# Merged expert and scan block of layer 2: key and decay rows spread to 128 partitions by transfers, value and query spreads of two steps in one round

## What is computed

```
x = x + L2_attn(xn) + L2_ffn(xn)
# L2_attn, per head and for every pair (i, j) of the 8 x 8 state, over the sequence:
state[t] = keep[t] * state[t-1] + (gate[t] * k[t])_i * v[t]_j
y[t]_j  = sum_i q[t]_i * state[t]_ij
# L2_ffn, per expert:
out = square(relu(x @ c_fc[e])) @ c_proj[e]
```

## Time and profile before

| | |
|---|---|
| median of the runs (lowest, highest) | 2280.9 us (2278.33, 2287.1) |
| profiled execution, its own time | 2283.21 us |
| its span | 2281.3 us |
| mean granted TensorE clock | 0.91 |
| busy share of the span: PE, DVE, ACT, POOL | 84%, 73%, 54%, 23% |
| merged block, first matmul to the next block's first | 1295.6 to 1518.7 us |

### The profile page before, as it was taken

How to read it: one execution, slowest core, us unless ns; L and a number is a source line. 1 busy time by engine, 2 the same in 40 slices (tenths; PEclk the granted TensorE clock), 3 DMA queues, 4 the chain that set the end, 5 groups by cost and what they waited for, 6 DMA issues and landing times. The chain is left out here.

```text
span 2281.3 us, 45278 instructions
## 1 busy us (share of the span) xinstructions
PE 1918.8 (84%) x17589; PEld 991.8 (43%) x17589; DVE 1669.8 (73%) x2861; ACT 1221.0 (54%) x2473; POOL 517.9 (23%) x602
## 2 busy tenths in 40 slices
PE   2888877866647999999978899999897988697899
PEld 1222221443211337943342377766443455565554
DVE  5999999685779996579854755537675887685665
ACT  3999999332324884368854255555342031184433
POOL 1112110012674551134425533320100000001100
PEclk7898999987776999999988899999998999987999
DMA  8423420100642524624211122220124242000000
GB/s 276 84 56 84 84 56 1 74 18 6 152 165 39 126 44 120 189 56 78 31 22 56 58 66 65 63 97 1 62 91 128 82 118 73 8 1 27 1 19 19
DMA packets 150333, 159.39 MB, mean 70 GB/s; under 512 B 53580, under 2 KB 123030, under 8 KB 150114
## 3 DMA queue, kind: packets, MB, share of 16 engines
q1 hardware_dynamic: 139880, 140.43, 22.7%
q0 software_dynamic: 10240, 16.06, 3.2%
HBM read 87.53 MB, written 72.82 MB: 70 GB/s over the span
## 5 line engine op out<-in xcount | busy, mean ns | idle before, releaser
L435 ACT ACTIVATE a_E<-a_scores,a_nmax 128x512 f32<-128x512 f32 x512 | 343.2, 814 | 14.6 <-DVE a_nmax L368 13.7
L1014 ACT ACTIVATE a_E<-a_scores 128x512 f32<-128x512 f32 x512 | 273.5, 601 | 96.4 <-PE a_scores L1049 91.3
L368 DVE TENSOR_REDUCE a_nmax<-a_scores 128x2 f32<-128x1024 f32 x256 | 302.6, 1217 | 21.8 <-PE a_scores L450 18.1
L918 DVE TENSOR_REDUCE a_nmax<-a_first 128x2 f32<-128x1024 f32 x256 | 295.5, 1217 | 15.2 <-PE a_first L1039 14.1
L450 PE MATMUL a_scores<-a_Vh,a_Kh 48*128 48x512 bf16 x512 | 108.2, 421 | 96.5 <-ACT a_E L435 71.9
L1039 PE MATMUL a_first<-a_Kh,a_Qh 48*128 48x512 bf16 x512 | 148.1, 416 | 36.9 <-PEq L51 20.1
L463 PE MATMUL a_turn<-a_E,a_QS 128*32 128x256 f32 x2048 | 174.1, 416 | 2.3 <-DVE a_QS L378 1.8
L435 ACT ACTIVATION_READ_ACCUMULATOR a_E<-a_scores,a_nmax 128x1 f32 x512 | 167.1, 335 | 0.0
L1049 PE MATMUL a_scores<-a_Qh,a_Kh 51*128 51x512 bf16 x512 | 160.7, 394 | 5.1 <-PEq L51 1.9
L1071 PE MATMUL a_out<-a_E,a_V 128*32 128x256 f32 x2048 | 161.7, 396 | 0.0
L450 PEld LDWEIGHTS a_scores<-a_Vh,a_Kh 48*128 48x128 bf16 x512 | 24.9, 94 | 216.5 <-ACT a_E L435 179.1
(11 more groups left out here) (546 smaller groups left out, 4409.4 us busy)
## 6 DMA issues: line engine op xcount, KB each, us to landing
f_up<-in_L_up SPq DMA_DIRECT2D x32, 256.0 KB, 3.3
a_Kh<-a_rows_k SPq DMA_DIRECT2D x16, 384.0 KB, 6.3
a_Vh<-a_rows_v SPq DMA_DIRECT2D x16, 384.0 KB, 9.8
a_Qh<-a_rows_q SPq DMA_DIRECT2D x32, 192.0 KB, 5.1
a_Kh<-a_rows_k SPq DMA_DIRECT2D x32, 192.0 KB, 6.1
slots<-empty SPq DMA_DIRECT2D x8, 645.0 KB, 6.4
f_xe<-slots SPq DMA_DIRECT2D x40, 129.0 KB, 2.0
outs<-zeros SPq DMA_DIRECT2D x8, 512.0 KB, 5.8
```

The costliest lines, as they stand in the source:

```text
L368: v.tensor_reduce(nmax[:, rd % 2, r1, :, q], bank(b, u)[:], AX.X, ALU.max, negate=True).then_inc(S["max_ready"], 1)
L435: m = a.activation(E[:, u % NE, x], bank(b, u)[:, x], ACT.Exp, bias=nmax[:, rd % 2, r1, x, q:q + 1], accum_out=Z[:, rd % 2, r1, x, q:q + 1])
L918: v.tensor_reduce(out, slot_bank(n)[:], AX.X, ALU.max, negate=True).then_inc(S["slot_read"], 1)
L1014: a.activation(E[:, u % NE, x], ps_s[n % 3][:], ACT.Exp, scale=SCALE).then_inc(S["exp_ready"], 1)
```

## The change

- The spreads of key and decay by TensorE go, with ScalarE's copy of the key and its three buffers, and the PSUM tiles ps_k and ps_d.
- SyncE issues a transfer for each in their place, `expand(i)`. It reads 16 rows of gk (or keep) in SBUF, each eight times, and writes 128 partitions of 512 float32. The destination is the array g.XT, which has no other use at this time: columns 0 to 3 of NB for keys, 4 to 7 for decays, so there are NX = 4 buffers of each. `at` is the first of the 16 rows: 96, 0, 32, 64, 112, 16, 48, 80 over the eight steps of a batch.
- The first four steps' transfers, eight in all, stand ahead of the wait for `put` and of the loads of tiles 0 and 1. After that, one pair (for step t+4) stands ahead of the load of tile t+3. The key's waits for product t (its buffer), the decay's for scan t.
- ps_v and ps_q have two buffers. On even s, TensorE spreads q(s), v(s+1), q(s+1), v(s+2) in one round; on odd s it spreads nothing.
- VectorE's product and scan take key and decay from SBUF, in place of a2m_gk_e and PSUM.

```diff
+                def expand(i):
+                    if i < ALL:
+                        b, t = first + i // NT, ORDER[i % NT]
+                        at = 32 * ((t // 2 + 3) % 4) + 16 * (t % 2)
+                        if i % NT == 0 and b >= GATED_EARLY:
+                            sp.wait_ge(S["gated"], b - GATED_EARLY + 1)
+                        if i >= NX:
+                            sp.wait_ge(S["kv_done"], i - NX + 1)
+                        sp.dma_start(key_rows[:, i % NX], mix["gk"][at:at + 16, b].unsqueeze(1).broadcast_to([16, 8, T])
+                                     ).then_inc(key_at[i % NX], 16)
+                        if i >= NX:
+                            sp.wait_ge(S["scanned"], i - NX + 1)
+                        sp.dma_start(decay_rows[:, i % NX], mix["keep"][at:at + 16, b].unsqueeze(1).broadcast_to([16, 8, T])
+                                     ).then_inc(decay_at[i % NX], 16)
+
+                for i in range(NX):
+                    expand(i)
                 sp.wait_ge(put, 16 * 2 * NB * R)
                 load(0)
                 load(1)
                 ahead(sp)
                 load(2)
                 for t in range(TILES):
+                    expand(t + NX)
                     load(t + 3)
...
                 for s in range(TILES):
-                    if s < ALL:
-                        spread_dq(s)
+                    if s % 2 == 0:
+                        spread_q(s)
                         spread_v(s + 1)
-                        spread_k(s + 2)
+                        spread_q(s + 1)
+                        spread_v(s + 2)
...
-                        v.tensor_tensor(kv[:, i % 2], gk_e[:, i % 3], ps_v[:], ALU.mult).then_inc(S["kv_done"], 1)
+                        v.tensor_tensor(kv[:, i % 2], key_rows[:, i % NX], ps_v[i % 2][:], ALU.mult).then_inc(S["kv_done"], 1)
...
-                    v.tensor_tensor_scan(state[:, i % NS], ps_d[:], kv[:, i % 2], 0.0, ALU.mult, ALU.add
+                    v.tensor_tensor_scan(state[:, i % NS], decay_rows[:, i % NX], kv[:, i % 2], 0.0, ALU.mult, ALU.add
                                          ).then_inc(S["scanned"], 1)
```

More of the change, by code:

```diff
@@ L2105, in experts_and_scan2 @@
         hr = k.sb("f2_hr", [128, 2, NF, TS])
-        gk_e, kv = k.sb("a2m_gk_e", [128, 3, T]), k.sb("a2m_kv", [128, 2, T])
+        kv = k.sb("a2m_kv", [128, 2, T])
+        NX = NB // 2
+        key_rows, decay_rows = g.XT[:, 0:NX], g.XT[:, NX:2 * NX]
+        key_at, decay_at = ([g.sem(f"f2m_{n}_at{i}") for i in range(NX)] for n in ("key", "decay"))
         NS = NT + 1
         state = k.sb("a2m_state", [128, NS, T])
-        ps_k, ps_v, ps_d, ps_q = (k.ps(f"a2m_ps_{n}", [128, T]) for n in "kvdq")
+        ps_v, ps_q = ([k.ps(f"a2m_ps_{n}{i}", [128, T]) for i in range(2)] for n in "vq")
         ps_x, ps_y = k.ps("f2_ps_x", [128, T]), k.ps("f2_ps_y", [128, T])
@@ L2112, in experts_and_scan2 @@
         S = {n: g.sem(f"f2m_{n}") for n in ("x_turned", "xT_ready", "h_done", "r_ready", "h_ready", "y_done", "y_ready",
-                                            "gated", "k_spread", "v_spread", "expanded", "k_read", "kv_done", "scanned",
+                                            "gated", "v_spread", "kv_done", "scanned",
                                             "state_ready", "picked", "sum_read", "q_spread", "row_ready")}
@@ L2160, in spread, with spread_q @@
                     return pe.matmul(ps[:], sel[rows, t % 2], mix[name][rows, b], start=True, stop=True)
[L2162 to L2169, removed]
                 def spread_v(i):
                     if i < ALL:
[L2173 to L2181, removed]
+                        if i >= 2:
+                            pe.wait_ge(S["kv_done"], i - 1)
+                        spread(ps_v[i % 2], "v", selJ, i, 1).then_inc(S["v_spread"], 1)
+                def spread_q(i):
+                    if i < ALL:
+                        if i >= 2:
+                            pe.wait_ge(S["state_ready"], i - 1)
+                        spread(ps_q[i % 2], "q", selI, i, 0).then_inc(S["q_spread"], 1)
                 def add_up(b):
@@ L2245, in _ @@
             def _(a):
[L2246 to L2249, removed]
-                            a.wait_ge(S["kv_done"], i - 2)
-                        a.copy(gk_e[:, i % 3], ps_k[:]).then_inc(S["k_read"], 1)
                 def sum_out(b):
@@ L2271, in out @@
                     a.copy(ye[:, t % 2].rearrange("p h c -> p (h c)"), ps_y[:, 0:2 * C]).then_inc(S["y_ready"], 1)
-                copy(0)
-                copy(1)
                 for s in range(TILES):
-                    copy(s + 2)
                     if s % NT == 0 and 0 < s <= ALL:
@@ L2292, in product @@
                     if i < ALL:
-                        v.wait_ge(S["k_read"], i + 1)
+                        v.wait_ge(key_at[i % NX], (i // NX + 1) * 16)
                         v.wait_ge(S["v_spread"], i + 1)
@@ L2296, in product @@
                             v.wait_ge(S["scanned"], i - 1)
-                        v.tensor_tensor(kv[:, i % 2], gk_e[:, i % 3], ps_v[:], ALU.mult).then_inc(S["kv_done"], 1)
+                        v.tensor_tensor(kv[:, i % 2], key_rows[:, i % NX], ps_v[i % 2][:], ALU.mult).then_inc(S["kv_done"], 1)
                 def scan(i):
-                    v.wait_ge(S["expanded"], i + 1)
+                    v.wait_ge(decay_at[i % NX], (i // NX + 1) * 16)
                     v.wait_ge(S["kv_done"], i + 1)
@@ L2309, in weigh @@
                     v.wait_ge(S["q_spread"], i + 1)
-                    v.tensor_tensor(state[:, i % NS], state[:, i % NS], ps_q[:], ALU.mult).then_inc(S["state_ready"], 1)
+                    v.tensor_tensor(state[:, i % NS], state[:, i % NS], ps_q[i % 2][:], ALU.mult).then_inc(S["state_ready"], 1)
                 def take(t):
```

2 lines of the change are left out of this document (removed).

## The result

The changed kernel takes 2325.6 us (median of 4 runs, 2316.8 to 2329.4), the kernel before 2284.0 us beside it: a ratio of 1.0177, 95% interval 1.0150 to 1.0203, so 41.6 us slower. The profiled execution took 2327.34 us, with a span of 2325.5.

The account below looks back on a forecast made before the run. TensorE's work was taken to bound the merged block. Rounds -21.4, start +13.0 and shortage +9.0 summed to +0.6 us on 2283.2, giving 2283.8; the median, 2.3 us lower, was forecast at 2281.5 us, range 2258 to 2311.

Parts of the forecast that it names:

- Rounds: TensorE's spread rounds in the merged block: 20 instead of 40, each 1.07 us, saving 21.4 us; mean step 4.66 us.
- Transfer: One key or decay transfer reading 16 SBUF rows: 2.28 us at 115 GB/s, between bounds of 0.72 and 4.7 us.
- Start: At the merged block's start, eight transfers stand before tile 0's load, so its turn comes 13.0 us late.
- The shortage in steady steps: Transfers plus other traffic exceed a step by 1.00 us; a quarter, 0.25 us, is lost over 36 steps: 9.0 us.
- SyncE's queue: Two more issues of 0.49 us each step before the load of tile t+3; the queue is not held longer.
- The bound rival: Transfers of 2.28 us bound the merged block without overlap: steps of 5.66 us, 36.0 us lost, 2308.5 us; chance 0.32.
- (1): Sign in the merged block: 20 rounds of 1.07 us and odd steps of 3.93 us where nothing waits.
- (2): Sign at the block's start: first turn some 13 us after 1303, with TensorE waiting for the load of xe.
- (3): Sign on the pairs: issue to landing over 4 us, growing where the queue backs up; under 3 us if hidden.
- (4): Sign in the merged block: a DMA share near 1, from 0.24.
- (5): Sign in the merged block: TensorE's waits for xe or the scan's for its decay sum to about 9 us.
- the remote 4.7 us: Remote case: a transfer takes 4.7 us by rate per source partition, a step 10.5 us, some 200 us slower; chance 0.03.

Follow-up runs that it names:

- The HBM version: The change with gk and keep stored to HBM, spreads read from there, first eight issued a block earlier; 2294.6 us, ratio 0.9858 to the kernel before.

## Why the prediction was wrong

It named the parts and mis-sized one, and half of what it missed there was not the transfers' rate but the place of another load behind them. Against +42.7 us in the block stood +0.6 in the sum, and 2325.6 us lie above the range's upper end of 2311. The rival that the transfers bound the block came nearest, 2308.5 us, and it too was 17 us short.

**Rounds, -21.4 us: right.** With a wide source two steps take 8.73 us; the pace is 4.57 to 4.63 in six kernels without a shortage (forecast: 4.66); the block with 128 rows is 21.5 us shorter than before. Copy, relu and scan were covered, as priced.

**Transfer, 2.28 us: too low.** It takes 2.70 where nothing moves beside it, 97 GB/s in place of 115. I had halved the 230 GB/s of a copy between 32 rows and 32, which was itself worked out from engines 70.0% occupied. The 32-row source gave 192 here, and half of that is what 16 rows give. So halving with the source came out right on average, and the value that I halved was too high. That it did so is in part luck: 16 rows eight apart are half as many too, and they lost nothing.

**Start, +13.0 us: about right, and in part by luck.** It is 14.4 to 14.5 us. By the prediction's own working 8 x 2.70 = 21.6 us of data would have brought the turn at 1296.7 + 21.6 + 1.2 = 1319.5, counted from the block's start of the kernel before; in the changed kernel the block began 2.8 us earlier, so 1316.7 is to be set against the turn at 1314.72. Two things make up the 2 us. The eight transfers moved at 103 GB/s over their first 12 us, since some neighbours overlap, and not at 97: 20.4 us of data in place of 21.6. And the load of xe, which was issued only at 1309.11 when the backed-up queue took it, landed beside the last transfer ahead of it and not behind it: that one was issued at 1306.61 and landed 7.8 us later, 0.3 us before the turn. The 0.8 us of landing in the sum stands on no row, and with 0.4 us of data it doesn't agree with the 0.9 us taken for the same thing at the data's beginning.

**The shortage in steady steps, +9.0 us: the step that failed.** The prediction had "I take a quarter of the shortage, 0.25 us, for the 36 steps", 9.0 us: measured were 49 us, 40.5 of them TensorE's waits for xe. Three things are in that.

- The full shortage is larger than 1.00 us, since a transfer is longer: 5.4 + 1.1 - 4.66 = 1.84 us a step. Of it 5.92 - 4.66 = 1.26 us were paid, two thirds in place of a quarter, if it is reckoned as the prediction did. "Successive steps read other quarters of the partitions" was the reason for so much overlap. But the two transfers that follow each other in the queue are the pair's, and they read the same quarter; and another quarter helps only if it lies in the other half, as the single microseconds above show. With the decay from the other half the pace falls to 5.17.
- The shortage was the sum of the pair and the other traffic. With xe on its own queue these two overlap, and the pair's time alone, 2 x 2.61 us against a step of 4.66, comes near the pace of 5.27. So the rate accounts for about half of the loss, and the place of the xe load for the rest.
- "SyncE's queue" was priced at two issues of 0.49 us. They take 2.5 and 0.6 us, and the xe load behind them 2.2; I read that as the queue being full, since the issues are short again in every kernel with quicker transfers or fewer. "The load has until late in step t+2, two steps or 9.3 us" was true for the landing alone. With xe on another queue half of the steady loss is gone, and the kernel is level with the one before. The bound rival names late tile loads but prices only the engines' time: 5.66 us a step, 36.0 us in all.

**Marks.** (1) Rounds of 1.07 us hold where nothing waits. (2) The turn came at 1314.72 with TensorE waiting for xe, 11.7 us after 1303.06 by the clock and 14.5 in the block. (3) Landing 5.6 to 8.9 us: as announced for the backed-up queue. (4) The DMA share is 0.87. (5) The waits are not 9 us but 54.9 on TensorE, 40.5 of them behind the start. Steps of a steady 5.92 us were named as the mark by which the forecast would be wrong, "then the transfers bound"; so it is, with the addition that what is bound first is the load behind them.

**The range** ended at 2311 because the bounds of the unknown cost were cut to 36 us, the whole shortage at 2.28 us. But 2.28 was the chosen value and not an end: between it and the remote 4.7 us nothing was priced. At 2.70 us with nothing overlapping it is 36 x 1.84 = 66 us, and with the start's 14.5 us some 2340 us would have been the end of the range.

**What stays open.** Why a narrow source leaves room for other traffic, and why the place of the xe load then costs 0.65 us a step and not more or less, was not tried by itself. What the lower clock behind the waits costs was not taken apart either. The pace with xe on its own queue is 5.27 with the pairs in place and 4.96 with the first ones issued earlier; that the backlog of the start lasts into the steps is argued, not shown. The HBM version was not run without the earlier issue, so its share of the 26 us is read from the pace alone (5.94 to 4.57).

## What to carry to other kernels

Before work is moved from an engine to transfers, work out the rate from where the source rows lie in SBUF, and set bytes over that rate plus the traffic that is there against the step; if it doesn't fit, store the rows to HBM once, from all partitions, and spread from there. A slow transfer holds its queue and the engine that issues it, so a load with a deadline belongs on another queue than the slow ones or in front of them. Where the price of an unmeasured transfer is chosen between bounds, the rival on the slow side must be worked out with a longer transfer too, not only with less overlap.

## What was not expected of the hardware

- For the same number of source rows the rate went with their position: 16 adjacent rows 97 GB/s, 16 rows eight apart 191. It was 192 for 32 adjacent ones and 347 for 128. From HBM, 16 rows repeated eight times showed no such limit (254 GB/s over 7 us). Neighbours in the queue overlap where they read different halves: 135 against 103 GB/s over 12 us.
- The issue of a transfer is held while those ahead of it are slow: 465 ns at the median with a quick source, 556 with half the narrow bytes, 2505 in the change. It reaches a load of another kind behind it as well, 326 ns for xe with the wide source:

```profile
L2128 SPq DMA_DIRECT2D f_xe<-slots x40: 325/326/1600, 1337.6 to 1512.6; - x40
```

and 2220 in the change.
- A DMA share of 0.81 cost nothing (32 rows, pace 4.57), one of 0.87 went with 1.26 us lost a step. The share says that the engines are occupied, not that somebody waits.
